# A spiking attention and a mixture of experts on one core: projections that begin with half of the tiles transposed, and a routing cut into parts

## The chip, the core and the metric

One core of one Trainium2 chip runs the whole program. The time is that of the device for one execution, in microseconds; where several runs are shown, their median counts. TensorE (PE in the profile) multiplies, VectorE (DVE), ScalarE (ACT) and GpSimd (POOL) do the elementwise work, and SyncE (SP) issues most of the transfers. Each engine goes through its own instructions in program order; semaphores tie the engines together.

## What is computed

The input is 2 x 2048 rows of 256 numbers. With `xn` the rows after a layer norm:

```python
x = L0_attn_query
xn = _layernorm(x, axis=-1)
x = x + _L0_attn_ref(xn, Wq, bq, ..., scale) + _L0_ffn_ref(xn, router_w, up_proj, down_proj)
```

The attention makes Q, K and V as spikes (1 where the layer norm of a projection is at least 1, else 0), weighs them by a Hamming distance and a bias by position, and makes spikes again after an output projection. The other branch routes each row to the 2 best of 8 experts by `xn @ router_w.T`, runs `silu(h[:256]) * h[256:]` and a down projection in each, and adds the two results, weighted.

## The kernel before

The 4096 rows are 32 tiles of 128 rows. The program goes through four stages.

**Prologue.** SP loads x in five chunks (`X_CHUNKS`: tiles 0-3, 4-7, 8-15, 16-23, 24-31). DVE takes means and variances of a chunk (`stats`), POOL the reciprocal deviation (`first_rstd`), DVE normalises the tiles in place (L807). PE transposes two tiles at a time (`turn_pair`, L1156) into one of four PSUM banks, ACT copies them out (`keep_xT`, L404). The router's logits are taken four tiles at a time, transposed (`logits`, L1168), copied (`keep_lgT`) and turned back (L1184). Beside this the four weight matrices `w_f` are prepared: POOL subtracts a base row (L646), ACT sums each half column block (`sum_weights`, L416), DVE subtracts the mean and multiplies by the sign of the gain (L828), and ACT and DVE split each number into an upper and a lower part (`w_h` L426, `w_l` L841), since every product is made of three matmuls (`three`, L1136 to L1138). The order is fixed: all 32 tiles are normalised, then the weights are signed, then the projections start.

**Projections.** Step t of 32 projects tile t to q, k and v: 3 groups of 6 matmuls (`project`). ACT takes the squares of each group (`squares`, L486) and, once for a pair of tiles, a square root (`deviations`, L492); DVE refines it (L988 to L994), makes six spikes (L1005) and splits the transposed tiles (`keep_xl`, L815; ACT's part is `keep_xh`). Four steps later PE turns tile t's q spikes (`turn_q`, L1202), ACT copies them (`keep_qT`, L478), and PE adds the product of k and v spikes to a bank (`sum_kv`, L1221). A PSUM bank holds two groups, and the pairs alternate between two sets of three banks.

Expert weights come in 24 pieces of 256 KB (`load_piece`, `ew_f`, two buffers); ACT writes a piece's upper part (L449), then POOL (the first 8, L643) or DVE (the others, L982) the lower part, which frees the buffer for the load after next.

**The routing** is DVE work ahead of the first pair's spikes: the best and second best expert (`pick` twice, L864 to L882), PE's counts and ranks by two matmuls, running counts and places (L887 to L919), then the gates (`set_gates`, L924 to L930) after the first pair. With places and gates set, POOL sends every tile's rows to two slots each in HBM: `scatter`, 64 indirect transfers (L683), each tile's pair waiting for the projections of three tiles on (`LEAD`). The rest of POOL's program stands behind them.

**Attention** runs over 16 blocks a of two tiles: PE sums near and far blocks, turns the spikes, and projects them; POOL takes a reciprocal deviation for each block (`out_rstd`, L703, and L687 for seven small scatters of padding between); DVE makes the output spikes (`spike_out`) and adds x (`add_x`). SP loads x again (`xo`, four slots, L354), loads the last ten pieces, and stores each block (`store_block`, L348); a slot is loaded again when its store has landed.

**Experts.** 71 tiles of 128 slots are loaded, projected up and down and added to the output by indirect transfers (L736).

The line that gates the scatters, and the loop behind it:

```python
            for t in range(NT):
                pool.wait_ge(s["proj_done"], G3 * min(t + LEAD, NT - 2))
                scatter(t)
            ...
            for a in range(NB):
                out_rstd(a)
```

## Time and profile before

| | us |
|---|---|
| median of 3 runs | 422.99 (421.54 to 424.07) |
| the profiled execution | 421.92 |
| its span | 420.1 |
| PE busy | 367.0 (87%) |
| DVE busy | 270.8 (64%) |
| POOL busy | 233.4 (56%) |
| ACT busy | 225.8 (54%) |

The profiled execution took 1.8 us more than its span and 1.07 us less than the median of the runs. Spans are counted from the first instruction; the busy times are sums over an engine's instructions and say nothing of what waits for what. For that the trace of each engine is read in order of time, with the start of each instruction in its first column.

### The profile page before, as it was taken

What the parts mean: (1) busy time and instruction counts of PE and PEld (TensorE: products, weight loads), DVE (VectorE), ACT (ScalarE), POOL (GpSimd) and SP (SyncE); (2) the same over time, 40 slices, a digit from 0 to 9 for tenths busy, and PEclk for the clock granted to TensorE, in tenths of its full rate; (3) what the DMA queues carried; (4) which work ended last, traced back from release to release, by engine and by line L of the source; (5) the groups of instructions that cost most, each with busy time, mean ns of one, the idle gap of its engine ahead of it and who ended that gap; (6) DMA issues with size and microseconds to landing.
All of it is one profiled execution on the core that took longest, in us unless ns stands there. A gap on an engine that the chain in (4) does not pass through costs nothing.

```text
span 420.1 us, 9186 instructions
## 1 busy us (share of the span) xinstructions
PE 367.0 (87%) x2429; PEld 297.0 (71%) x2430; DVE 270.8 (64%) x897; ACT 225.8 (54%) x716; POOL 233.4 (56%) x207
## 2 busy tenths in 40 slices
PE   5198876999999989998979999999999999999980
PEld 1033676888888847665767888888888788888860
DVE  4699799987777646757775555555555555555540
ACT  1456774777777645534454555555555555555540
POOL 4547424777777753542335755464755555555652
PEclk9689978999999999998999999999999999999995
DMA  7943012244626323557455757565666656565643
GB/s 258 322 153 75 26 50 65 102 154 128 206 103 217 113 90 114 190 189 219 133 162 171 114 97 110 91 103 99 101 101 101 99 90 97 96 100 94 104 52 37
DMA packets 43460, 51.72 MB, mean 123 GB/s; under 512 B 6342, under 2 KB 37064, under 8 KB 43432
## 3 DMA queue, kind: packets, MB, share of 16 engines
q0 software_dynamic: 13952, 19.30, 26.2%
q1 hardware_dynamic: 27488, 30.21, 24.1%
q10 hardware_dynamic: 1992, 1.89, 1.4%
q8 instruction: 12, 0.20, 0.2%
q14 instruction: 16, 0.13, 0.1%
HBM read 27.89 MB, written 23.48 MB: 122 GB/s over the span
## 4 chain that ended last, share of the span: by engine, by line
PE 51%; DVE 19%; DMA 14%; ACT 6%; issue 5%; SPq 1%; POOLq 0%; DVEq 0%; POOL 0%; ACTq 0%
PE bank L1136 14%; PE bank L1138 13%; PE bank L1137 13%; DMA out<-xo 7%; DMA xn<-x 3%; PE bank L1278 3%; DVE qk_spk L1005 3%; PE bank L1260 3%; DVE xn L807 2%; DMA ew_f<-experts 2%; ACT junk L486 2%; DVE xst L785 2%; PE bank L1312 2%; DMA ex<-slot_x 2%; DVE exT_l L974 2%
## 5 line engine op out<-in xcount | busy, mean ns | idle before, releaser
L736 POOL DMA_INDIRECT out<-ey,dest x71 | 110.0, 1549 | 78.9 <-DMA out<-ey,dest 24.4
L1036 DVE TENSOR_TENSOR hid<-gact,bank 128x256 f32<-128x256 f32 x71 | 29.9, 421 | 76.7 <-ACT gact L531 76.7
L683 POOL DMA_INDIRECT slot_x<-xn,pos x64 | 62.8, 982 | 25.7 <-issue 19.3
L1136 PE MATMUL bank<-ew,exT_h 128*128 x142 | 62.1, 437 | 6.4 <-DVE exT_l L974 6.2
L1136 PE MATMUL bank<-w_h,xT_h 128*128 128x256 f32 x192 | 58.9, 307 | 0.3 <-DVE w_l L841 0.3
L531 ACT ACTIVATE gact<-bank 128x256 f32<-128x256 f32 x71 | 27.3, 384 | 57.2 <-PE bank L1138 57.2
L1137 PE MATMUL bank<-w_l,xT_h 128*128 128x256 f32 x192 | 56.3, 293 | 0.0
L1138 PE MATMUL bank<-w_h,xT_l 128*128 128x256 f32 x192 | 56.1, 292 | 0.0
L1138 PE MATMUL bank<-ew,exT_l 128*128 x142 | 55.9, 394 | 0.0
L1137 PE MATMUL bank<-ew,exT_h 128*128 x142 | 55.8, 393 | 0.0
L486 ACT ACTIVATE junk<-bank 128x256 bf16<-128x256 f32 x96 | 35.9, 380 | 27.7 <-PE bank L1138 27.4
L1136 PE MATMUL bank<-ew,hidT_h 128*128 x142 | 46.0, 324 | 2.1 <-DVE hidT_l L1040 2.0
L541 ACT ACTIVATE hidT_h<-bank 128x256 fp32r<-128x256 f32 x71 | 27.2, 384 | 34.6 <-PE bank L1278 34.5
L1138 PE MATMUL bank<-ew,hidT_l 128*128 x142 | 40.3, 284 | 0.0
L1137 PE MATMUL bank<-ew,hidT_h 128*128 x142 | 40.2, 283 | 0.0
L1136 PEld LDWEIGHTS bank<-w_h,xT_h 128*128 128x128 f32 x192 | 38.7, 202 | 0.6 <-issue 0.4
L703 POOL TENSOR_TENSOR rstd<-veps,neg_half 128x2 f32<-128x2 f32 x16 | 17.0, 1061 | 39.6 <-DVE veps L1073 39.6
L1137 PEld LDWEIGHTS bank<-w_l,xT_h 128*128 128x128 f32 x192 | 38.8, 202 | 0.0
L1138 PEld LDWEIGHTS bank<-w_h,xT_l 128*128 128x128 f32 x192 | 38.8, 202 | 0.0
L1136 PEld LDWEIGHTS bank<-ew,exT_h 128*128 128x128 f32 x142 | 26.7, 188 | 13.7 <-issue 10.6
L547 ACT ACTIVATE ey<-bank,gate 128x256 f32<-128x256 f32 x71 | 33.2, 468 | 2.6 <-PE bank L1138 1.5
L1040 DVE TENSOR_TENSOR hidT_l<-bank,hidT_h 128x256 fp32r<-128x256 f32 x71 | 30.1, 424 | 6.6 <-ACT hidT_h L541 2.9
(203 smaller groups left out, 893.3 us busy)
## 6 DMA issues: line engine op xcount, KB each, us to landing
ex<-slot_x SPq DMA_DIRECT2D x71, 130.0 KB, 2.6
ew_f<-experts SPq DMA_DIRECT2D x24, 256.0 KB, 3.2
xo<-x SPq DMA_DIRECT2D x16, 256.0 KB, 3.0
out<-xo SPq DMA_DIRECT2D x16, 256.0 KB, 3.5
xn<-x SPq DMA_DIRECT2D x6, 512.0 KB, 12.6
out<-ey,dest POOLq DMA_INDIRECT x71, 3.9
xn<-x SPq DMA_DIRECT2D x4, 256.0 KB, 3.8
w_f<-w_all ACTq DMA_DIRECT2D x1, 1024.0 KB, 8.1
```

Of the source, the lines that this page charges most:

```text
L486: nc.scalar.activation(junk[:, i % JUNK, :], proj_ps[r][i], ACT.Square, accum_out=ssq[:, r, i:i + 1]).then_inc(s["ssq_done"], 1)
L531: nc.scalar.activation(gact[:, m % 2, :], h_ps[m % 2][:, 0:F], ACT.Silu).then_inc(s["gact_done"], 1)
L541: nc.scalar.activation(flat2(hidT_h[:, m % 2, :, :]), hT_ps[m % 2], ACT.Copy).then_inc(s["hidh_set"], 1)
L547: nc.scalar.activation(ey[:, m % 4, :], y_ps[m % 2], ACT.Copy, scale=gate[:, m % 4:m % 4 + 1]).then_inc(s["ey_done"], 1)
L683: pool.indirect_dma_start(slot_x, bass.IndirectOffsetOnAxis(ap=pos[:, k, t:t + 1], axis=0), xn[:, t, :], None).then_inc(s[done], 16)
L703: g.tensor_tensor(rstd[:, a % 2, 0:B], veps[:, a % 2, 0:B], neg_half[:, 0:B], ALU.pow).then_inc(s["w_rstd"], 1)
L736: pool.indirect_dma_start(out, bass.IndirectOffsetOnAxis(ap=dest[:, j:j + 1], axis=0), ey[:, j % 4, :], None, compute_op=ALU.add).then_inc ...
L1036: v.tensor_tensor(hid[:, m % 2, :], gact[:, m % 2, :], h_ps[m % 2][:, F:2 * F], ALU.mult).then_inc(s["hid_done"], 1)
L1040: v.tensor_tensor(flat2(hidT_l[:, m % 2, :, :]), hT_ps[m % 2], flat2(hidT_h[:, m % 2, :, :]).bitcast(F32), ALU.subtract).then_inc(s["hidl_ ...
L1136: mm(dst, a_h, b_h, start=first, stop=False)
L1137: mm(dst, a_h, b_l, start=False, stop=False)
L1138: return mm(dst, a_l, b_h, start=False, stop=last)
```

## The change

The prologue now turns 16 tiles only (`AHEAD = 8` pairs); pairs 8 to 15 are transposed and routed inside steps 1 to 4 of the projections, two pairs a step, all through one bank (6). DVE signs the weights in two halves between the chunks' statistics and subtracts the base itself; the signs are spread by one DVE instruction (128x1024) and two matmuls rather than a transfer. The normalisation of tiles 12-15, 20-23 and 28-31 goes to POOL, that of tiles 24-27 to ACT. The logits are taken for one tile at a time, with the transposed tile as the stationary side, straight into bank 7. The routing is cut into seven parts: with `PICKED = 2`, `pick_first` stands behind pair 2's spikes on DVE, `pick_second` behind pair 3's, `counts` behind pair 4's, `places` and `set_gates` behind pair 5's, the rest behind pairs 6 and 7. Bank 7 is used for the routing until then, so the key sums begin at step 15 with the first 12 tiles in two steps. The scatters have no wait of their own any more. DVE's refinement of the square root has three instructions in place of four. The pieces come in another order (`ORDER`, `PIECES_AT`).

```diff
-LGT_PIECE, BIAS_PIECE, RT_PIECE, XT_PIECE = 9, 13, 15, 17
+ROUTING_PIECES, BIAS_PIECE, RT_PIECE, XT_PIECE = range(9, 13), 13, 15, 17
+ORDER = [*range(POOL_PIECES), 8, 14, 16, 17, 18, 19, 9, 10, 11, 12, 13, 15, 20, 21, 22, 23]
...
-LEAD = 3
...
+PIECES_AT = {0: 0, 2: 1, 4: 2, 5: 3, 6: 4, 7: 5, 8: 6, 9: 7, 12: 8, 14: 9, 16: 10, 18: 11, 20: 12, 22: 13}
+LATE = [t for t, m in PIECES_AT.items() if m >= POOL_PIECES]
+ATTENTION_PIECES = {k: len(PIECES_AT) + k for k in range(PIECES - len(PIECES_AT))}
 FIRST_ROWS = 9
+AHEAD = 8
+PICKED = 2
+TURNS_FROM = 1
+OPENED = 15
+EARLY_K = 12
+POOL_NORM = [t for t in range(X_CHUNKS[2][0], NT) if t % 8 >= 4]
+ACT_NORM = [t for t in range(X_CHUNKS[4][0], NT) if t % 8 < 4]
...
+        x_ps = [banks[i % 4 if i < AHEAD else 6] for i in range(NT // 2)]
+        sgn_ps = [part(4 + g // 2, g % 2) for g in range(G4)]
+        lg_ps = banks[7][:, 0:NT * E]
...
+            for i in range(4):
+                keep_xT(i)
+            for i in range(KC * G4):
+                sum_weights(i)
+            act.wait_ge(s["bias_in"], 32)
+            sum_biases()
             halve_weights(1)
-            keep_lgT(NT // RG - 1)
+            keep_xT(4)
+            keep_xT(5)
+            halve_weights(0)
+            keep_xT(6)
+            keep_xT(7)
+            keep_xh(0)
+            keep_xh(1)
+            halve_out_weights()
+            halve_biases()
 
...
+                if 0 <= t - TURNS_FROM < 4:
+                    keep_xT(AHEAD + 2 * (t - TURNS_FROM))
+                    keep_xT(AHEAD + 2 * (t - TURNS_FROM) + 1)
...
+                if t in PIECES_AT:
+                    piece_upper(PIECES_AT[t])
                 if not even:
                     act.wait_ge(s["proj_done"], G3 * t + 3)
                     squares(t, 4)
-                    if t == 1:
+                    deviations(t)
...
+                if t == 1:
+                    normalise()
...
+            def normalise(c):
+                for t in [t for t in POOL_NORM if X_CHUNKS[c][0] <= t < X_CHUNKS[c][1]]:
+                    g.tensor_scalar(xn[:, t, 0:D], xn[:, t, 0:D], xmean[:, t:t + 1], xrstd[:, t:t + 1],
+                                    ALU.subtract, ALU.mult).then_inc(s["xn_pool"], 1)
...
+            set_ones(0)
+            set_ones(1)
+            for c in range(2, len(X_CHUNKS)):
                 first_rstd(c)
-            piece_lower(0, 0)
-            first_rstd(len(X_CHUNKS) - 1)
-            for n in range(1, POOL_PIECES):
-                if n < 4:
-                    set_ones(n - 1)
-                if n == 4:
-                    for group in range(3, NT // RG):
-                        set_ones(group)
-                    pool.wait_ge(s["w_halved"], 2 * KC)
-                    g.tensor_tensor(wo_l[:, :, :], w_f[:, :, G3 * D:], wo_h[:, :, :].bitcast(F32), ALU.subtract).then_inc(s["wo_parted"], 1)
-                piece_lower(n, n)
+                pool.wait_ge(s["xrstd_done"], c + 1)
+                if c == len(X_CHUNKS) - 1:
+                    offsets(c)
+                normalise(c)
+                if c == 3:
+                    set_ones(2)
+                    set_ones(3)
+            pool.wait_ge(s["wo_halved"], KC)
+            g.tensor_tensor(wo_l[:, :, :], w_f[:, :, G3 * D:], wo_h[:, :, :].bitcast(F32), ALU.subtract).then_inc(s["wo_parted"], 1)
+            piece_lower(0)
+            for group in range(4, NT // RG):
+                set_ones(group)
+            for m in range(1, POOL_PIECES):
+                piece_lower(m)
...
             for t in range(NT):
-                pool.wait_ge(s["proj_done"], G3 * min(t + LEAD, NT - 2))
                 scatter(t)
...
+            stats(0)
+            stats(1)
+            normalise(0)
+            normalise(1)
+            dve.wait_ge(s["w_in"], 16)
+            dve.wait_ge(s["base_in"], 16)
+            subtract_base(1)
+            dve.wait_ge(s["row0_gone"], 1)
+            subtract_base(0)
+            stats(2)
+            sign_weights(1)
+            normalise(2)
+            stats(3)
+            sign_weights(0)
...
+            for i, c in enumerate((1, 0)):
+                dve.wait_ge(s["w_halved"], i + 1)
+                v.tensor_tensor(w_l[:, c, :], w_f[:, c, 0:G3 * D], w_h[:, c, :].bitcast(F32), ALU.subtract).then_inc(s["w_parted"], 1)
...
+            normalise(3)
+            stats(4)
+            normalise(4)
+            keep_xl(2)
+            keep_xl(3)
...
+                for at, part_of_routing in enumerate((pick_first, pick_second, counts, places, set_gates, rest_of_routing, landings)):
+                    if pair == PICKED + at - (at >= 4):
+                        part_of_routing()
...
+                turned = AHEAD + 2 * (t - TURNS_FROM)
+                turning = TURNS_FROM <= t < TURNS_FROM + 4
+                if turning:
+                    turn_pair(turned)
+                    logits(turned - 1)
                 for i in range(t % 2 * G3, (t % 2 + 1) * G3):
+                    if turning and i % G3 == G3 - 1:
+                        turn_pair(turned + 1)
+                        logits(turned)
...
+                if t == TURNS_FROM + 4:
+                    logits(NT // 2 - 1)
+                for at in range(t - 3) if t == TURNS_FROM + 4 else range(t - 4, t - 3) if t > TURNS_FROM + 4 else ():
+                    turn_q(at, at)
...
+                if t == 2 * PICKED + 6:
+                    counts()
+                if t == 2 * PICKED + 8:
                     ranks()
-                if m == 4:
+                if t == OPENED:
                     open_kv()
-                if not early(t, 4):
-                    sum_kv(t - 4, m - 4)
+                first = (t - OPENED) * EARLY_K // 2 if t < OPENED + 2 else t - 4
+                for at in range(first, min(first + EARLY_K // 2, t - 3) if t == OPENED else t - 3) if t >= OPENED else ():
+                    sum_kv(at, at)
```

What stands where, word for word in program order, at three places. First DVE behind the spikes of a pair (`qk_spk`, `qT`, `v_spk` in L1005, now L1056, are the spikes; `xT_l` is `keep_xl`; `first`, `second`, `work`, `best` are the picks; `cnt` and `run_c` the counts, `slot_of` and `pos` the places). Before, the whole routing up to the places stands ahead of the first pair:

```order
L882 TENSOR_TENSOR gwork<-best 128x32
L815 TENSOR_TENSOR xT_l<-xT,xT_h 128x256 [waits xh_set]
L887 COPY cnt<-bank 128x256 [waits ranked]
...
L919 CAST pos<-pos_f 128x64 [waits dve_order]
L988 TENSOR_SCALAR veps<-ssq 128x6 [waits ssq_done,wo_parted,w_parted]
L990 RECIPROCAL inv_std<-std 128x6 [waits std_done]
...
L1005 SCALAR_TENSOR_TENSOR qk_spk<-thr_r,std,bank 128x256 x2
L924 TENSOR_SCALAR gwork<-gwork 128x32 [waits gate_exp,bias_set]
```

Now, behind the spikes of pair 5:

```order
L1056 SCALAR_TENSOR_TENSOR qk_spk<-thr_r,std,bank 128x256 [waits q_turned]
L1056 SCALAR_TENSOR_TENSOR qT<-thr_r,std,bank 128x256
L961 TENSOR_TENSOR slot_of<-bank,run_c 128x256 [waits dve_order,ranked]
...
L969 CAST pos<-pos_f 128x64 [waits dve_order]
L974 TENSOR_SCALAR gwork<-gwork 128x32 [waits gate_exp]
...
L980 TENSOR_TENSOR xn<-gwork,xn 128x32 [waits dve_order]
L1033 TENSOR_TENSOR ew<-ew_f,ew 128x512 [waits piece_h]
```

The places (`pos`) and gates moved from the first pair to the sixth.

Second, POOL ahead of and behind the 64 scatters. Before:

```order
L676 TENSOR_TENSOR wo_l<-w_f,wo_h 128x512 [waits w_halved]
L643 TENSOR_TENSOR ew<-ew_f,ew 128x512 [waits piece_h] x4
L683 DMA slot_x<-xn,pos 9088x260 [waits proj_done,gates_set,placed]
L683 DMA slot_x<-xn,pos 9088x260
L683 DMA slot_x<-xn,pos 9088x260 [waits proj_done]
```

Now:

```order
L691 TENSOR_TENSOR wo_l<-w_f,wo_h 128x512 [waits wo_halved]
L665 TENSOR_TENSOR ew<-ew_f,ew 128x512 [waits piece_h]
L672 MEMSET xT 1x4x128 [waits logits_done] x3
L672 MEMSET xT_v 1x2x128 [waits logits_done]
L672 MEMSET xT_q 1x2x128
L665 TENSOR_TENSOR ew<-ew_f,ew 128x512 [waits piece_h] x7
L702 DMA slot_x<-xn,pos 9088x260 [waits gates_set,placed]
L702 DMA slot_x<-xn,pos 9088x260 x63
L721 TENSOR_TENSOR rstd<-veps,neg_half 128x2 [waits w_var,pads_marked,pads_placed]
```

Four more memsets that wait for logits now stand between the first and the second piece, and the scatters wait only once.

Third, PE in step 1, between the groups of a tile (`id_f,xn` is a transposition, `w_rt,xT` the logits):

```order
L1188 MATMUL bank<-w_h,xT_l 128x256
L1220 MATMUL bank<-id_f,xn 128x128 [waits xn_done,xT_ready]
L1220 MATMUL bank<-id_f,xn 128x128
L1220 MATMUL bank<-id_f,xn 128x128 [waits xn_done]
L1220 MATMUL bank<-id_f,xn 128x128
L1228 MATMUL bank<-w_rt,xT 128x8 [waits xT_ready]
L1228 MATMUL bank<-w_rt,xT 128x8 x3
L1186 MATMUL bank<-w_h,xT_h 128x256
```

The second pair of each of these steps waits for ACT's copy of the first (`xT_ready`), which ACT does behind the squares of the group before it.

## Rows read from the trace of the kernel before

**Rows 1.** PE, first group of projection matmuls by line: min/median/max ns, first and last start.

```profile
L1136 PE MATMUL bank<-w_h,xT_h x192: 278/283/579, 50.0 to 147.2; 128*128 128x256 f32 x192
```

**Rows 2.** POOL's scatters: busy and idle by group; idle by cause; first scatter; first out_rstd.

```profile
L683 POOL DMA_INDIRECT slot_x<-xn,pos x64 | 62.8, 982 | 25.7 <-issue 19.3
...
  issue: 19.3, 47
...
71.46 1.09 POOL L683 DMA_INDIRECT slot_x<-xn,pos  x1 [5.24 <-issue]
...
162.37 0.73 POOL L703 TENSOR_TENSOR rstd<-veps,neg_half 128x2 f32<-128x2 f32 x1 [7.59 <-DVE veps L1073]
```

**Rows 3.** SP in the attention, timeline: first store of a block; last load of xo.

```profile
166.23 0.39 SPq L348 DMA_DIRECT2D out<-xo  x1
...
216.90 0.37 SPq L354 DMA_DIRECT2D xo<-x  x1
```

**Rows 4.** DVE in the prologue, timeline (start us, us).

```profile
16.66 2.71 DVE L785 BATCH_NORM_STATS2 xst<-xn 128x6 f32<-128x256 f32 x8 [3.72 <-DMA xn<-x]
...
20.42 1.38 DVE L807 TENSOR_SCALAR xn<-xn,xmean,xrstd 128x256 f32<-128x256 f32 x4
...
42.08 3.26 DVE L828 SCALAR_TENSOR_TENSOR w_f<-w_f,w_mean,sgn_r 128x256 f32<-128x256 f32 x8
...
48.76 0.96 DVE L841 TENSOR_TENSOR w_l<-w_f,w_h 128x768 fp32r<-128x768 f32 x1 [0.56 <-ACT wo_h L427]
```

**Rows 5.** PE, timeline: transpositions of four tiles; logits of four tiles.

```profile
39.21 1.09 PE L1156 MATMUL bank<-id_f,xn 128*128 128x128 f32 x8
40.23 1.88 PE L1168 MATMUL bank<-xT,w_rt 128*8 128x512 f32 x4
```

**Rows 6.** PE in a window of two us: busy (count), granted clock, DMA share, GB/s.

```profile
52.00:54.00 2.00, 2.00 (x12) 0.50 0.00 0
```

**Rows 7.** Steady steps: PE's turns of q; ACT's squares and its copy; two xT copies.

```profile
100.78 0.27 PE L1202 MATMUL bank<-id_b,qk_spk 128*128 128x128 bf16 x2 [0.51 <-DVE qk_spk L1005]
...
103.21 0.27 PE L1202 MATMUL bank<-id_b,qk_spk 128*128 128x128 bf16 x2
...
99.52 0.38 ACT L486 ACTIVATE junk<-bank 128x256 bf16<-128x256 f32 x1 [0.31 <-PE bank L1138]
...
100.25 0.38 ACT L478 ACTIVATE qT<-bank 128x256 bf16<-128x256 bf16 x1
...
26.72 1.25 ACT L404 ACTIVATE xT<-bank 128x512 f32<-128x512 f32 x2 [0.45 <-PE bank L1156]
```

**Rows 8.** Pieces: their load (KB, us to landing); POOL's lower parts, timeline.

```profile
ew_f<-experts SPq DMA_DIRECT2D x24, 256.0 KB, 3.2
...
53.66 2.52 POOL L643 TENSOR_TENSOR ew<-ew_f,ew 128x512 fp32r<-128x512 f32 x2 [2.80 <-ACT ew L449]
```

**Rows 9.** DVE, timeline: a later pair without routing, its first and last group.

```profile
88.51 0.17 DVE L988 TENSOR_SCALAR veps<-ssq 128x6 f32<-128x6 f32 x1
...
91.45 0.87 DVE L1005 SCALAR_TENSOR_TENSOR qk_spk<-thr_r,std,bank 128x256 bf16<-128x256 f32 x2
```

**Rows 10.** DVE, timeline: the routing's parts, by their first and last instructions.

```profile
51.48 0.42 DVE L864 TENSOR_REDUCE best<-bank 128x32 f32<-128x256 f32 x1
...
58.31 0.42 DVE L815 TENSOR_TENSOR xT_l<-xT,xT_h 128x256 fp32r<-128x256 f32 x1
59.06 0.42 DVE L887 COPY cnt<-bank 128x256 f32<-128x256 f32 x1 [0.33 <-PE bank L1194]
...
64.63 0.38 DVE L919 CAST pos<-pos_f 128x64 int32<-128x64 f32 x1
...
70.34 0.22 DVE L930 TENSOR_TENSOR xn<-gwork,xn 128x32 f32<-128x32 f32 x1
```

**Rows 11.** ACT, timeline: the table load ahead of a square root, and the root.

```profile
58.67 1.28 ACT L492 ACT_TABLE_LOAD   x1
59.97 0.30 ACT L492 ACTIVATE std<-ssq,eps_c 128x6 f32<-128x6 f32 x1
```

More of the change, by code:

```diff
@@ L1146, in _, with wait_normal @@
             pe.wait_ge(s["ident_in"], 16)
+            pe.wait_ge(s["ones_set"], 1)
+            pe.wait_ge(s["sgn_put"], 1)
+            signs = sgn_w[:, :, :].rearrange("p a j -> p (a j)")
+            for h in range(2):
+                last = mm(banks[4 + h][:, :], ones_b[:, :], signs[:, h * G4 * D // 2:(h + 1) * G4 * D // 2], start=True, stop=True)
+            last.then_inc(s["sgn_set"], 1)
+            def wait_normal(t):
+                for who, done in ((POOL_NORM, "xn_pool"), (ACT_NORM, "xn_act")):
+                    if t in who:
+                        pe.wait_ge(s[done], who.index(t) + 1)
+                        return
+                pe.wait_ge(s["xn_done"], t + 1 - sum(n < t for n in POOL_NORM + ACT_NORM))
             def turn_pair(i):
-                if i >= 4:
+                if i > AHEAD:
+                    pe.wait_ge(s["xT_ready"], i)
+                elif 4 <= i < AHEAD:
                     pe.wait_ge(s["xT_ready"], i - 3)
@@ L1187, in ranks @@
-            def ranks():
-                pe.wait_ge(s["const_in"], 32)
-                pe.wait_ge(s["ones_set"], 1)
-                pe.wait_ge(s["chosen_set"], 1)
-                picks = chosen[:, :, :].rearrange("p t e -> p (t e)")
-                mm(rank_ps[:, 0:NT * E], before_s[:, :], picks, start=True, stop=True)
-                mm(rank_ps[:, NT * E:], ones_b[:, :], picks, start=True, stop=True).then_inc(s["ranked"], 1)
+            for i in range(4):
+                turn_pair(i)
+                if i >= 1:
+                    logits(i - 1)
@@ new lines, in _, with counts @@
+            logits(3)
+            for i in range(4, AHEAD):
+                turn_pair(i)
+                if i >= 5:
+                    logits(i - 1)
+            def counts():
+                pe.wait_ge(s["const_in"], 32)
+                pe.wait_ge(s["chosen_set"], 1)
+                mm(lg_ps, ones_b[:, :], chosen[:, :, :].rearrange("p t e -> p (t e)"), start=True, stop=True).then_inc(s["counted"], 1)
+            def ranks():
+                pe.wait_ge(s["counts_kept"], 1)
+                mm(lg_ps, before_s[:, :], chosen[:, :, :].rearrange("p t e -> p (t e)"), start=True, stop=True).then_inc(s["ranked"], 1)
```

363 lines of the change are left out of this document (162 added, 201 removed).

## The prediction

> **What bounds the kernel now.** I read the chain of waits first: it goes through DVE's prologue, then through PE and DVE in the projections, then through SP's stores in the attention, then through PE in the experts. Next I read each engine in order of time around the three seams between stages. The first projection starts at 50.0 us and the last group at 147.2 [rows 1]. Whatever happens before is prologue, and this change is about the prologue. But the row that decides is POOL's. Its 64 scatters start at 71.5. Their busy time is 62.8 and the idle time before them 25.7, of which 5.24 stands ahead of the first: 62.8 + 25.7 - 5.24 = 83.3 us from the first start to the last end, 154.8 [rows 2]. POOL's next work is the first `out_rstd` of the attention at 162.37, 7.6 us later, and DVE releases it, not POOL. So the scatters have 7.6 us to spare, no more. From there SP carries the end: the first block is stored at 166.23, and each of the following blocks waits until a slot's store has landed, until the last load of x at 216.90 [rows 3]. The experts stand behind that and nothing in them changes. So the time moves by as much as `out_rstd` of block 0 moves: it needs both the end of the projections (147.2 + 15.2 = 162.4) and the end of the scatters.
>
> **The start of the projections.** Before, statistics of chunk 2 start at 16.66, when its x has landed, and take until 20.42: 3.76 us for 8 tiles; four normalisations take 1.38 [rows 4]. DVE now has the spread of the signs, eight normalisations and two subtractions ahead of these statistics. By hand the spread costs 1.2 us (an estimate, from 0.96 for 768 columns [rows 4] to 1024) and each subtraction about that 0.96; with POOL's memset between them it all fits before 17.4. Then, in DVE's order: statistics 3.8, signs of one half 1.9 (8 took 3.26 [rows 4], and two small steps), normalisation of four tiles 1.4, statistics 3.8, signs 1.9, bias 0.6, two lower parts 1.9, one `keep_xl` 0.4. 17.4 + 15.7 = **33.1** for the first projection, 16.9 us earlier than 50.0. ACT's sums and copies and PE's 16 transpositions lie beside this. POOL normalises four tiles in between: no row shows that instruction; half of a 128x512 lower part is 0.63, twice of it 2.5 [rows 8], and even at 2.5 each the four end at 33, just in time.
>
> **Steps 0 to 5.** A step is 18 matmuls, a turn of q and two key sums: 103.21 - 100.78 = 2.43 us [rows 7], thus some 0.12 for a matmul, 0.72 for a group, 2.16 for a tile. Early in the projections of before, the granted clock was 0.50, 1.2 in place of 2.4 GHz, with 12 matmuls started in 2 us [rows 6]; step 0 now starts behind some idle microseconds of PE, and I take that level for most of it. Tile 0 then takes 3.5. In steps 1 to 4 PE adds two pairs of transpositions at 0.55 (8 in 1.09) and two logits. These are a new form: four matmuls of 8 columns against a 128x128 tile. From below they cost nothing beyond loads like the transpositions', 0.5; from above four of the old form, 1.88 [rows 5]; I take 0.5, since the load is the same and the moving side is small. More costly is the wait in the middle. The second pair goes into the same bank as the first, so it waits for ACT: end of a group 0.3, two squares 0.73 (99.52 to 100.25), one copy 0.6 (two in 1.25) [rows 7], with two hand-overs 1.8. An odd step has one group before that, an even one two: 0.55 + 0.5 + 0.72 + 1.8 + 0.55 + 0.5 + 0.72 = 5.3 and 6.1. Four steps: 22.8. Step 5 opens with one logits and two turns of q, the second behind ACT's copy of the first: 3.5. So tile 5 is done at 33.1 + 3.5 + 22.8 + 3.5 = 62.9, and a further 0.8 for ACT's own four normalisations. Its root is set 1.4 later, at 65.1.
>
> One more thing is queued. SP's load of piece 3 waits for POOL's lower part of piece 1, which now stands behind memsets that wait for the last logits, in step 5 (about 60.5). Memset, lower part 1.3, load 3.2, upper part 0.6 [rows 8]: ACT gets to the end of that piece at about 66.5, and two squares and the root of pair 2 stand behind it on ACT, 1.0: **67.5** in place of 65.1.
>
> **From there to the gates.** DVE now has more than PE. A pair without routing costs it 3.7 us (88.51 to 92.3 less the instruction dropped [rows 9]). Pairs 2 to 5: 14.8. The two picks cost 6.8 (51.48 to 58.31), counts and places 5.6 (59.06 to 65.0, less the `keep_xl` inside), the gates 1.0, ended by 70.34 before [rows 10]. Together 28.2, so the gates are set at 67.5 + 28.2 = **95.7**. PE's 2.43 a tile would take 20 us for the eight tiles, so PE waits for DVE there. In the kernel before the same point was 71.5 [rows 2]: the projections start 17 us earlier, the scatters 24 us later.
>
> **The scatters** no longer wait for projections. 17 of 64 did; their idle time was 25.7 - 19.3 = 6.4, of which 5.1 is the gap of 0.3 that all others have too (19.3 for 47, 5.24 of it the first [rows 2]). So 83.3 - 1.3 = 82.0 us at least. 95.7 + 82.0 = 177.7, against 162.4: **15.3 later**. The projections end earlier than before, near 144 (tile 13 at 91, 18 more at 2.8 as from 50.0 to 147.2 minus the slow start, 3 for the key sums moved), which would have let block 0 go at 159, but it now waits 18 us for POOL.
>
> **After the wait** the block's other work is ready, which saves 0.9 between `out_rstd` and its store (3.9 before, 162.37 to 166.23). PE is held at block 2's output projection and may come back at half clock [rows 6] for some us, which costs about 1 on block 2's store. DVE's chain for the root has still three instructions behind ACT's root; one is dropped that was done in ACT's shadow: nothing. SP's chain behind the first store is bound by stores that land, and is the same. Sum: 421.9 + 15.3 - 0.9 + 1 = 437.3 for an execution like the profiled one, which lies 1.07 under the median of the runs. I say **437**.
>
> **A rule weighed.** ACT's exponential for the gates now stands between the roots of pairs 4 and 5, so a table is loaded for it and one for the next root. The row shows 1.28 for a load and the root begins at 59.97, right behind its end at 59.95 [rows 11]. The root of pair 5 then comes just as DVE gets to it, and the sum is as above. The Trainium skill, "ScalarE: Activation LUTs", section "What ACT_TABLE_LOAD costs", gives 1283 ns for the load and about 1380 ns of drain besides. By that rule the root would come 1.4 later and the gates about 1 us later, and the time with them; the trace disagrees on the drain.
>
> **Rivals.**
> 1. *Faster: POOL issues quicker than it did.* If the gap between scatters goes with the waits, each takes its 0.98 and 64 take 63. Then they end at 159, the end of the projections decides, and the time is 422 - 3 = 419. It decides from a pace under 1.03 us each, (162.4 - 95.7) / 64. Against it: 47 scatters that waited for nothing had the gap [rows 2]. A faster routing alone gives little: even at PE's pace throughout (tile 5 at 56, eight tiles in 20, root and routing 5) the gates come at 81, with no gain at all. Chance 0.13, for both together.
> 2. *No change.* The gates come at 79 to 82: steps 1 to 4 without the wait for ACT (-7), the piece in time (-2.4), the picks at less (-1), and DVE's routing in gaps of its own. Too many at once: 0.07. The time would be 421 to 425.
> 3. *Much slower.* The half clock comes back after each of the waits of 1 to 2 us in steps 1 to 13, since PE is idle a quarter of that time. With tiles at 3.8 in place of 2.16 for half of ten tiles, the gates are 8 later: 445. Against it: steps with a gap of 0.51 ran at full speed, 2.43 [rows 7]; what wider gaps do, no row here shows. Chance 0.15.
> 4. *The forecast*, POOL's scatters as the bound with gates from 88 to 101: 0.65, 429 to 443.
>
> **Numbers.** The difference that a measurement can tell from none is 0.5%, 2.1 us. Faster by more: rival 1, 0.13. Within: 0.07. Slower: 0.80. The range must leave out no more than 2 in 10: it starts at 426, above rivals 1 and 2, which hold 0.2, and goes to 446, through rival 3.
>
> **What would show it.** First projection near 33; steps 1 to 4 near 5.3 and 6.1 with PE waiting on ACT's xT; scatters from 95 to 177 with no waits; the first reciprocal of the attention right behind the last scatter, PE idle some 15 us before; SP's chain from first store to last load still about 51. If POOL idles before its first `out_rstd`, or the first scatter is before 82, the forecast is wrong.

## The result, and the profile after

The changed kernel takes **445.95 us** (median of 4 runs, 444.31 to 449.89); the kernel before, beside it, 423.38. The ratio is 1.055, 95% interval 1.047 to 1.063. (Ratios here are those on record, taken over the executions of the faster of two states and not from the medians, so they can differ from the medians' quotient by up to 0.004.) The direction was forecast, the size was not: 437.0 was said, with a range to 446.0. The time just fills it, and the ratio applied to the 422.99 from which the forecast started gives 446.4, just above it. In a second comparison it took 445.79 against 422.67, ratio 1.052 (1.046 to 1.058). The profiled execution has a span of 443.1 us (444.92 with what lies around it).

The page's busy shares and granted clock, in 40 slices of 11.1 us:

```profile
PE   6878779688799983199797999999999999999971
POOL 3289615206777777746234565556565555555652
PEclk9557998999999999589999999999999999999995
```

In slices 16 and 17 (from 166 us) PE sinks to 3 and 1 while POOL goes on at 7: PE has finished the projections and waits. The groups of POOL's scatters and of PE's projections (times: min/median/max ns, first and last start us):

```profile
L702 POOL DMA_INDIRECT slot_x<-xn,pos x64 | 63.7, 995 | 37.9 <-issue 19.2
...
L702 POOL DMA_INDIRECT slot_x<-xn,pos x64: 956/960/1470, 101.4 to 183.3; - x64
...
L1186 PE MATMUL bank<-w_h,xT_h x192: 278/283/561, 35.7 to 150.4; 128*128 128x256 f32 x192
```

Against [rows 2] the scatters start at 101.4 in place of 71.5, and the last starts at 183.3, 29.5 us later than before (153.8); against [rows 1] the projections start 14.3 earlier and end 3.2 later. So more than the whole head start is gone by their end. The chain that ended last, at the seam (start us, us):

```profile
183.31 0.96 POOL slot_x L702
184.29 0.74 POOL rstd L721
185.03 0.19 issue
185.22 1.04 POOL slot_x L706
```

The first `out_rstd` (L721) stands at 184.29, right behind the last scatter and with no wait for DVE, whose `veps` for it was there at 167.3. Before, it stood at 162.37 behind 7.59 us of idle time. SP's loads and stores in the attention, first and last start:

```profile
L360 SPq DMA_DIRECT2D xo<-x x16: 367/368/442, 160.8 to 238.2; - x16
...
L354 SPq DMA_DIRECT2D out<-xo x16: 383/445/1218, 187.3 to 244.3; - x16
```

From first store to last load of x it is 50.9 us, as before (50.7 [rows 3]). ACT between the root of pair 0 and the routing (the roots are L504):

```profile
46.24 0.30 ACT L504 ACTIVATE std<-ssq,eps_c 128x6 f32<-128x6 f32 x1
...
58.96 0.30 ACT L504 ACTIVATE std<-ssq,eps_c 128x6 f32<-128x6 f32 x1
...
69.99 0.63 ACT L464 ACTIVATE ew<-ew_f 128x512 fp32r<-128x512 f32 x1 [1.36 <-DMA ew_f<-experts]
...
71.38 0.30 ACT L504 ACTIVATE std<-ssq,eps_c 128x6 f32<-128x6 f32 x1
...
91.81 1.28 ACT L504 ACT_TABLE_LOAD   x1
93.10 0.30 ACT L504 ACTIVATE std<-ssq,eps_c 128x6 f32<-128x6 f32 x1
```

and DVE's last steps to the gates:

```profile
99.31 0.19 DVE L969 CAST pos<-pos_f 128x64 int32<-128x64 f32 x1
...
100.26 0.22 DVE L980 TENSOR_TENSOR xn<-gwork,xn 128x32 f32<-128x32 f32 x1
```

The picked pair's root comes at 71.38 and the gates are set at 100.5. That is the forecast's chain, each link later than it was said.

### The profile page after: what moved, and what is told of

The parts are those of the page before. It is cut to its first block, busy times and chain, and to the rows that moved or that the text cites. A ratio compares the mean times of both kernels' runs of the same rounds, so it can differ in the third digit from the quotient of the medians.

```text
span 443.1 us, 9273 instructions
## 1 busy us (share of the span) xinstructions
PE 373.7 (84%) x2483; PEld 316.0 (71%) x2492; DVE 263.4 (59%) x870; ACT 223.6 (50%) x712; POOL 246.8 (56%) x218
## 4 chain that ended last, share of the span: by engine, by line
PE 46%; POOL 19%; issue 13%; DVE 10%; ACT 4%; DMA 4%; POOLq 0%; SPq 0%; ACTq 0%; DVEq 0%
POOL slot_x L702 14%; PE bank L1186 13%; PE bank L1188 11%; PE bank L1187 11%; PE bank L1228 3%; POOL rstd L721 3%; PE bank L1347 3%; PE bank L1329 3%; PE bank L1220 2%; DMA ex<-slot_x 2%; POOL slot_x L706 2%; DMA out<-xo 2%; DVE exT_l L1024 1%; ACT gact L543 1%; DVE xst L807 1%
## 5 line engine op out<-in xcount | busy, mean ns | idle before, releaser
L754 POOL DMA_INDIRECT out<-ey,dest x71 | 109.6, 1544 | 80.6 <-ACT ey L559 24.4
L702 POOL DMA_INDIRECT slot_x<-xn,pos x64 | 63.7, 995 | 37.9 <-issue 19.2
L1186 PE MATMUL bank<-ew,hidT_h 128*128 x142 | 46.2, 325 | 2.0 <-DVE hidT_l L1090 2.0
L721 POOL TENSOR_TENSOR rstd<-veps,neg_half 128x2 f32<-128x2 f32 x16 | 17.0, 1061 | 31.6 <-DVE veps L1123 31.6
```

Of the source, the lines that this page charges most:

```text
L702: pool.indirect_dma_start(slot_x, bass.IndirectOffsetOnAxis(ap=pos[:, k, t:t + 1], axis=0), xn[:, t, :], None).then_inc(s[done], 16)
L721: g.tensor_tensor(rstd[:, a % 2, 0:B], veps[:, a % 2, 0:B], neg_half[:, 0:B], ALU.pow).then_inc(s["w_rstd"], 1)
L754: pool.indirect_dma_start(out, bass.IndirectOffsetOnAxis(ap=dest[:, j:j + 1], axis=0), ey[:, j % 4, :], None, compute_op=ALU.add).then_inc ...
L1186: mm(dst, a_h, b_h, start=first, stop=False)
```

## The experiments

### Is the late end of the scatters the whole loss?

**g3_lead15** takes the kernel *before* and delays nothing but its scatters:

```
-LEAD = 3
+LEAD = 15
```

> The kernel before, with one number changed: scatters of tile t wait for projection step t + 15 instead of t + 3, so that POOL's last scatter ends where the changed kernel's does (184.3 instead of about 155). Nothing else of the change is in it. Forecast's theory (the late end of POOL's scatters is the whole loss): out_rstd(0) at 184 to 186, time 443 to 447, ratio 1.05 to 1.055, as the changed kernel. Rival (scatters late is only a part, the rest is lost in the changed kernel's waits and clock): 430 to 438.

Measured: 444.39 against 422.81, ratio 1.051 (1.049 to 1.053). The first `out_rstd` came at 186.1 and the last load of x at 238.6, where the changed kernel has 238.2. A kernel with none of the change's edits, only with POOL's scatters as late, is as slow. Not to the microsecond: its `out_rstd` stands 1.8 us behind the changed kernel's and its median 1.5 below, so some 3 of the changed kernel's 22.6 us come from elsewhere. The rest of what the other edits gain and lose lies beside POOL.

**f0_after** is the changed kernel again, beside the three that follow.

> The changed kernel, unchanged, beside the kernel before. In the first comparison the ratio was 1.055. In the batch before this one three variants of it stood at 1.11 to 1.13 of the kernel before on the same chip, with TensorE and ScalarE idle for tens of us while POOL issued its scatters, and the wait ending on nothing that the profile shows. Theory A (the variants' edits do it): this run shows 1.055 and no such idle time. Theory B (it is a state of the chip, and hits whatever kernel has projections still to fetch beside scatters): on a chip with it this run too stands at 1.10 to 1.13; on a chip without it, 1.055.

Measured: 445.79, ratio 1.052 (1.046 to 1.058). By itself that fits both theories. What speaks against A is that e1_between's and e4_lump's very edits, which stood at 1.115 and 1.129, stand at 1.054 and 1.035 in the same comparison as this run (f1_between and f2_lump). Its profile comes below.

### Taking POOL off the path, and starting it earlier

**f1_between** puts the last 7 tiles' scatters and the pads between the first blocks' `out_rstd`:

```
+BESIDE = 7
...
-            for t in range(NT):
+            for t in range(NT - BESIDE):
                 scatter(t)
...
                 out_rstd(a)
-                if a < PC:
-                    scatter_pad(a)
+                if a < BESIDE:
+                    scatter(NT - BESIDE + a)
+                elif a < BESIDE + 3:
+                    for c in range(PC * (a - BESIDE) // 3, PC * (a - BESIDE + 1) // 3):
+                        scatter_pad(c)
```

> The changed kernel with its last 7 scatters of tokens, and then the pad rows' scatters, put between out_rstd(0) to out_rstd(9) on POOL instead of before out_rstd(0). Theory forecast (POOL's scatters end last): without stalls out_rstd(0) goes from 184.3 to about 170, and the time falls by 13 to 17 us, to about 0.965 to 0.97 of the changed kernel. Rival (expert loop waits for the last pads, so that the scatters are the bound wherever they stand): no change within 3 us.

Measured: 445.24 against 422.67, ratio 1.054 (1.050 to 1.058): nothing gained, although the first `out_rstd` stood at 168.8, 15.5 us earlier. SP's waits from 150 to 262 us (total, times, longest) tell why:

```profile
SPq L361 <- DMA out<-xo: 35.1, 11, 5.1
...
SPq L369 <- DMA slot_x<-pad_row,pad_i: 12.6, 1, 12.6
```

In block 9 SP waits for *all* scatters and pads before it loads the first slots, and the later blocks' loads of x are queued behind that wait. It stood there 12.6 us, and each of the six blocks left took a store's landing. The rival had the result right, with this queue as its reason.

**g1_between5** moves 5 tiles in place of 7, and that wait (`FIRST_ROWS`) from block 9 to 11.

> The changed kernel with its last 5 tiles of scatters (10 of 64) and the pad rows' scatters put between out_rstd(0) and out_rstd(7), and SP's wait for all scatters moved from block 9 to block 11, since in the run before (7 tiles, wait at 9) SP stood 12.6 us at that wait and the rest of the blocks went at 3.6 us each behind it. Theory (POOL's scatters end last, and SP's wait took back the gain): out_rstd(0) at about 172 instead of 184.3, the last load of xo at 228 or 229 instead of 238.2, time 9 to 10 us below the changed kernel. Rival (all of POOL's work has to be done before the expert loop wherever it stands): within 3 us of it.

Measured: 436.59 against 422.81, ratio 1.033 (1.030 to 1.037), 9 us less. `out_rstd` of block 0 at 171.4, last load of x at 229.2: the theory's numbers. Two things changed at once against f1_between; that the moved wait is the one that counts is read from SP's waits, in which none for the pads is left.

**f2_lump** leaves the scatters alone and has the whole routing in one piece behind step 7:

```
-                    if pair == PICKED + at - (at >= 4):
+                    if pair == PICKED + max(0, at - 4):
...
-                if t == 2 * PICKED + 6:
+                if t == 2 * PICKED + 3:
                     counts()
-                if t == 2 * PICKED + 8:
                     ranks()
```

(on ACT, the exponential goes from `2 * PICKED + 5` to `+ 3`.)

> The changed kernel with the routing not in parts: three routing steps (counts and ranks too) stand right behind step 7 instead of spread to step 12. On the disturbed chip the first scatter came at 93.8 instead of 101.4. Theory (start of the scatters sets the end): 7 to 9 us less, 437 for 446, as all that stands behind POOL's chain moves with it. Rival (what the projections lose by the lump comes back at the end): less than 3 us.

Measured: 436.85 against 422.67, ratio 1.035 (1.031 to 1.038), 9 us less. First scatter 93.1 for 101.4, first `out_rstd` 174.9 for 184.3.

**f3_both** and **g2_both5** join the lump with f1_between's and g1_between5's edits; f3_both has POOL's memsets of g4_ones (below) besides.

> Lump and between together, and POOL's memsets for groups 4 on behind the lower pieces of the experts' weights instead of before them. Theory: POOL is off the chain; out_rstd(0) then follows the projections (end at 150 + 15, 166 to 168), and the time is 424 to 430, about the kernel before, not below it, since step 1 still begins 15 us early and loses it at waits. Rival (start stretch given back): 415 to 420.

> The same with the routing in one lump, which alone gave 9 us. Theory: both gains add, out_rstd(0) at 165 to 167 (projections' end 152 + 15 is then as late), time 421 to 428, level with the kernel before. Rival: the two share one gain, 434 to 437.

Measured: 446.56, ratio 1.057 (1.052 to 1.063), and 436.03, ratio 1.028 (1.025 to 1.030). g2_both5 came out as its rival said: the gains share one limit. f3_both hit neither span (424 to 430, 415 to 420): SP stood 12.7 us at the same wait for the pads as in f1_between. ACT's last root of the projections in the changed kernel, in the lump, and in g2_both5:

```profile
L504 ACT ACTIVATE std<-ssq,eps_c x16: 298/299/302, 46.2 to 151.8; 128x6 f32<-128x6 f32 x16
```

```profile
L504 ACT ACTIVATE std<-ssq,eps_c x16: 298/299/301, 46.3 to 159.2; 128x6 f32<-128x6 f32 x16
```

```profile
L505 ACT ACTIVATE std<-ssq,eps_c x16: 298/299/303, 46.7 to 162.1; 128x6 f32<-128x6 f32 x16
```

The lump starves PE for DVE's 14 us of routing and ends the projections 7 to 10 us later. Alone that costs nothing, since POOL ends at 174.9 anyway; with POOL taken off the path the projections decide, and `out_rstd` of block 0 is back at 175.9, behind 10.5 us in which POOL waits for DVE. (The profiled execution of g2_both5 took 439.56, 3.5 more than the median; PE's granted clock was 0.50 to 0.66 in it from 50 to 62 us.)

### The steps ahead of the gates

**g4_ones** moves POOL's memsets for the later logits behind its lower parts (behind all eight of them; what counts is that pieces 1 and 2 are among these).

> The changed kernel, with POOL's memsets of the ones of groups 4 on put behind the lower parts of pieces 1 and 2 instead of before them, so that piece 3 lands earlier: ACT waited 1.36 us for it at 69.99, in the middle of the steps before the root of pair 2. Theory (the forecast's step on piece 3): the root of pair 2 and all behind it 1.4 to 2 us earlier, time 1 to 2 us less, ratio 1.047 to 1.051. Rival (the pair's root hangs on TensorE's steps alone): no change within 1 us.

Measured: 444.07 against 422.81, ratio 1.051 (1.047 to 1.056): inside the theory's span and, with this interval, no less inside the rival's. The trace decides: ACT's wait for piece 3 is gone and the root of pair 2 stands at 70.64 for 71.38, of which 0.27 was there at pair 0; ACT waits 0.93 for PE in its place. The late piece was real and worth half a microsecond.

**h1_picked1** sets `PICKED = 1`.

> The changed kernel with PICKED = 1 instead of 2: the routing's parts each stand one pair of steps earlier. Forecast's step (gates = root of the picked pair + 28.2, and all behind follows): a pair is 6 us, first scatter at 95 to 96 instead of 101.4, time 5 to 6.5 us below the changed kernel (439 to 441). Rival (the routing waits then for something else, as logits of the last tiles or the router's copies): first scatter moves by less than 3 us, and so does the time.

Measured: 440.26 against 422.32, ratio 1.041 (1.038 to 1.044), 5 us less, as the theory says; but in the profiled execution, the longest of its five, the first scatter came at 100.8, as the rival says. PE's clock was at half there from 50 to 60 us, which it was not in the changed kernel's profile. The time is measured; the way to it is not shown by this trace. h4_best's, below, has the first scatter at 97.8, 3.6 earlier, part of which is g4_ones' edit: less than the 5 to 6 of the theory.

**h2_warm** keeps PE busy in the prologue with 16 matmuls that nobody reads.

> The changed kernel with 16 matmuls 128x512 in the transposing stretch whose result nobody reads, to keep TensorE busy while it waits (6 before the transposes of pair 4, 4 before those of pair 6, 6 before step 0). Theory (TensorE's half clock from 12 to 38 us makes the late start): the granted clock is 1.00 before 30 us and the first projection comes 2 to 3 us earlier, at 33, time 2 to 3 us less. Rival (DVE and POOL set the pace there; the matmuls add or hide): the first projection stays at 35.6 within 1 us, the time within 1.5.

Measured: 447.43, ratio 1.060 (1.057 to 1.062). PE ran at 0.91 to 0.94 from 26 to 34 us, where it had 0.50, and the first projection came at 36.8, not at 35.7. The theory's 33 did not come, but that does not clear PE's clock. The clock rose too late: DVE's wait of 1.3 us for `xrstd`, which hangs on PE's logits (the first point under Wrong, below), was over at 24.4 and is as long as before. And the last six of the added matmuls themselves stand in front of the first projection, at a clock of 0.50 again (34 to 38 us). L1301 is their line, of which the trace has five:

```profile
34.97 2.34 PE bank L1301 x5
```

What the half clock costs at the start is not settled by this run.

**h3_dvenorm** sets `POOL_NORM = []`, so that DVE does all of POOL's normalisations.

> The changed kernel with the normalisation of all tiles on DVE (and ScalarE as before), none on POOL; DVE gets 12 more operations of 0.34 us, POOL loses 12 of 1.2 to 1.9 us (and one of 3.9). Theory (POOL's normalisation is on the path of the start): first projection 2 us earlier, time 2 us less. Rival (DVE is as full as POOL there, and gets 4 us more): first projection as late or later, time the same or 1 to 2 us more.

Measured: 454.17, ratio 1.076 (1.073 to 1.079), 9 us more: further than the rival said. The start is only 1.9 later (37.6). The profile is that of the longest of the six executions (461.93), and what PE's clock did in it comes next. The five others have no trace; their mean granted clock was 0.905 to 0.921, the changed kernel's four had 0.918 to 0.930. Where the median's further 7 us came from is open.

**h4_best** joins `PICKED = 1`, the memsets behind the pieces, and g1_between5's order.

> PICKED = 1, the memsets of ones behind the pieces, and the last 5 tiles' scatters and the pads' between out_rstd(0) and out_rstd(7). Theory: out_rstd(0) comes from 171.4 to the end of the projections + 15, 166 to 167, time 428 to 432; still above the kernel before, since the projections end 3 us later than its own (150.3 for 147.2) and the last blocks' loads keep their pace. Rival: POOL's remaining work bounds it again, 434 to 437.

Measured: **430.43** against 422.32, ratio 1.018 (1.014 to 1.022), the best version of the changed kernel. First scatter 97.8. The first `out_rstd` still stands right behind a scatter:

```profile
166.68 0.17 DVE L1126 TENSOR_SCALAR veps<-ssq 128x2 f32<-128x2 f32 x1 [1.61 <-ACT junk L587]
...
166.74 0.96 POOL L702 DMA_INDIRECT slot_x<-xn,pos  x1 [0.30 <-issue]
...
167.71 0.76 POOL L721 TENSOR_TENSOR rstd<-veps,neg_half 128x2 f32<-128x2 f32 x1
```

DVE's `veps` was there at 166.9, so without the scatter it would have gone some 0.6 us earlier. Both limits have come together: 167.7 is 16 us behind the last group of the projections (151.8), and in the kernel before, 162.4 is 15 behind 147.2. The projections end 4.6 later than there, and the last load of x comes 5.6 later (222.5).

### A spell at half clock

f0_after's profiled execution, the longest of its four, is the same program as the changed kernel's, but its span was 453.3, not 443.1. Windows of 4 us (busy time and count of PE, PEld, DVE, ACT, POOL; granted clock), first of the 443.1 us execution, then of the 453.3 us one, then of h3_dvenorm:

```profile
46.00:50.00 4.00, 2.09 (x18) 1.89 (x17) 0.13 (x1) 3.97 (x13) 4.00 (x5) 1.00 0.00 0
50.00:54.00 4.00, 3.93 (x35) 3.93 (x36) 3.90 (x11) 1.44 (x4) 1.84 (x3) 1.00 0.22 70
...
66.00:70.00 4.00, 3.96 (x23) 3.90 (x23) 3.29 (x3) 1.84 (x8) 2.44 (x2) 0.57 0.34 79
70.00:74.00 4.00, 3.21 (x29) 3.04 (x27) 2.18 (x8) 3.78 (x14) 1.41 (x2) 1.00 0.33 110
```

```profile
46.00:50.00 4.00, 2.76 (x24) 2.55 (x22) 0.00 (x0) 3.93 (x13) 4.00 (x4) 1.00 0.00 0
50.00:54.00 4.00, 3.27 (x17) 3.27 (x18) 3.36 (x9) 2.10 (x6) 2.13 (x3) 0.65 0.19 70
54.00:58.00 4.00, 4.00 (x21) 4.00 (x20) 1.43 (x4) 0.00 (x0) 0.51 (x1) 0.50 0.00 0
...
82.00:86.00 4.00, 3.36 (x30) 3.19 (x29) 3.55 (x11) 2.96 (x12) 0.99 (x2) 1.00 0.24 70
```

```profile
46.00:50.00 4.00, 1.62 (x11) 1.42 (x11) 3.94 (x9) 3.00 (x10) 2.45 (x2) 0.65 0.13 16
50.00:54.00 4.00, 4.00 (x20) 4.00 (x20) 2.16 (x6) 0.41 (x1) 0.51 (x1) 0.50 0.14 49
...
78.00:82.00 4.00, 4.00 (x21) 3.80 (x20) 0.00 (x0) 0.00 (x0) 0.10 (x1) 0.50 0.00 0
```

In the second the clock fell to 1.2 GHz behind ACT's four normalisations (46 to 50 us, in which PE waits) and stayed there until 82. PE starts some 20 matmuls in 4 us there where it starts up to 35 at full clock, and DVE and ACT stand idle for lack of work. The roots of pairs 0, 1 and 2 come at 46.9, 64.7 and 82.0 for 46.2, 59.0 and 71.4, the first scatter at 112.6 for 101.4, and the span is 10.2 longer. So the difference arises in this stretch, beside the clock. These are two single executions: why the clock fell in one and not in the other is not shown. In h3_dvenorm's the clock fell in the same place and was back only behind 86 us: first scatter 118.5. The kernel before has such windows too [rows 6], but its scatters started at 71.5 with 7.6 us to spare at the end.

### Two comparisons in which engines stood idle

The first four runs (e1 to e4) and the last two (i1, i2) fell in conditions under which the kernel before itself took 452.2 and 448.4 us; their times aren't comparable with the others, and only their traces up to the scatters are used.

> Theory (POOL's 64 scatters stand ahead of the first out_rstd and set the end): with the last seven tiles' scatters put behind out_rstd of blocks 0 to 6, block 0 waits for the end of the projections only, 150.4 + 15.2 = 166 in place of 184.3; time 446 - 18 = 428, up to 431 if POOL is then busy in every block. Rival (the projections lose the time themselves, the scatters only end at about the same moment): block 0 goes at 183 as before and the time stays within 1 of 446. Nothing but POOL's order is changed.

> The kernel before, with each tile's scatters held until 16 tiles on are projected in place of 3. Theory: the first scatter moves from 71.5 to about 93, the last ends 82 later at 175 in place of 154.8, the 7.6 of slack are used up, and out_rstd of block 0 goes at 175 to 176; time 422 + 13 = 435. Rival (the end of the projections decides and scatters are hidden): 423, within 0.5%.

> The changed kernel, with ACT copying a step's first pair ahead of the squares instead of behind them, so that PE's second pair in steps 1 to 4 does not wait. Theory: each of the four steps is 1.5 to 1.8 shorter, the root of pair 2 is 5 to 6 earlier, and so are the gates, the scatters and the end: 440. Rival (DVE or the piece queue behind the last logits decides, not this wait): 445 to 446.

> The changed kernel, with picks, counts, places and gates in one piece behind pair 2's spikes. Theory: the 28 us from the root to the gates lose three pairs' own work (3 x 3.7), so the gates come at 90 in place of 100.5 and the time is 435 to 436, although PE starves once for some 9 us. Rival (the end of the projections decides): PE's long wait costs as much as the short ones or more, 446 to 449.

Measured: 505.08, 472.79, 505.95 and 510.58 against 452.24. e1 and e4 are f1 and f2 above; e2 is g3 with 16 for 15. A window of e3 in the midst of the scatters:

```profile
140.00:150.00 10.00, 0.00 (x0) 0.00 (x0) 0.00 (x0) 0.00 (x0) 7.56 (x9) 0.50 0.29 107
```

POOL scatters at its pace while PE, DVE and ACT have no instruction at all from 130 to 160 us, and PE is busy for 1.9 us in the 50 from 120 to 170. What PEld waits for in i1, from 95 to 240 us:

```profile
PEld bank L1258 <- issue: 72.1, 5, 51.6
```

The wait ends on nothing that the profile shows, and what it is, no run here shows. It does not come with the scatters alone: f0 to h4, whose programs have the same scatters (h1 to h4 ran on the very chip of e1 to e4), had none of it. None of the times expected for these runs, i1 and i2 among them, came, and they say nothing for or against the theories.

e3 and i1 test the wait in the middle of steps 1 to 4, by ACT's first copy of xT ahead of the squares; i1 has g4's memsets besides, and i2 has `PICKED = 1` and g1's order too.

```
+                if 0 <= t - TURNS_FROM < 4:
+                    keep_xT(AHEAD + 2 * (t - TURNS_FROM))
                 if even:
```

> The changed kernel with ACT's first copy of xT of steps 1 to 4 ahead of the squares instead of behind them, and POOL's memsets of ones behind the lower parts of pieces 1 and 2, so that piece 3 is no longer late. Theory (the wait in the middle is on the path, and piece 3 hid its gain in the earlier run): root of pair 2 at 68 to 70 instead of 71.4, first scatter 2 to 3.5 us earlier, time 2 to 3.5 less than the changed kernel (ratio 1.045 to 1.048). Rival (TensorE's clock and work set the steps): first scatter within 1 us of 101.4, ratio 1.050 to 1.055.

> The same with PICKED = 1 and the last 5 tiles' scatters and the pads' between out_rstd(0) and out_rstd(7): the combination that gave 430.4, plus ACT's copies first. Theory: out_rstd(0) bound by the projections' end + 15, so 1 to 3 us less than that, 427.5 to 429.5. Rival: no change, 430 to 431. Below the kernel before (422.5) it does not come in either.

Measured: 503.62 and 494.00 against 448.38. In e3 the root of pair 2 came at 71.07, behind a wait of 1.85 us for piece 3. In i1, without that wait, at 68.77 for 71.38, and the first scatter at 99.5 for 101.4. Between e3 and i1 the piece is worth 2.3 us at the root, where it was worth half a microsecond alone (g4_ones). What the wait in the middle costs is not separated: PE's granted clock was 0.64 and 0.50 (e3), 0.60 and 0.55 (i1) in the two windows from 50 to 58 us and 1.00 from 66 to 70, where the changed kernel's had 1.00 and then 0.57. The whole, 2.6 us at the root and 1.9 at the scatters, is a little less than the theory. What it brings in time, and whether i2 beats 430.4, stays open.

## Why the prediction was right and wrong

**Right**: the mechanism and its place. [Rows 2]'s 7.6 us to spare, the 64 scatters without waits, PE idle at the seam, `out_rstd` right behind the last scatter, SP's chain of 51 us; g3_lead15 shows it to be the loss, all but some 3 us. Rival 1's condition did not come: the gap of 0.3 stayed (19.2 for 63), at 1.27 each. The store of block 0 came 3.0 us behind its `out_rstd`, the 0.9 less that was said. The table load had no drain behind it (91.81 + 1.28, root at 93.10) and none ahead of it (ACT's instruction before ended at 91.79). There the trace again disagrees with the Trainium skill's "ScalarE: Activation LUTs", section "What ACT_TABLE_LOAD costs".

**Wrong**: the size. The first `out_rstd` moved by 21.9, not 15.3. The steps that failed are terms of the sum up to the first scatter, by the table:

| step | forecast | measured | miss, summed |
| --- | --- | --- | --- |
| first projection | 33.1 | 35.7 | 2.6 |
| root of pair 2 | 67.5 | 71.4 | 3.9 |
| gates set | 95.7 | 100.5 | 4.8 |
| first scatter | 95.7 | 101.4 | 5.7 |
| end of the last scatter | 177.7 | 184.3 | 6.6 |

1. *The start of the projections*, 2.6 of 6.6, the largest. The forecast added up DVE's work, gave its hand-overs no time, and said that ACT's and PE's work "lie beside this". They don't. DVE's waits until then are:

```profile
DVE xn L829 <- POOL xrstd L650: 1.3, 1, 1.3
DVE w_f L833 <- POOL w_r L678: 0.8, 1, 0.8
DVE w_mean L837 <- ACT junk L426: 0.6, 1, 0.6
```

   The 0.8 lies ahead of the statistics of chunk 2, which start at 17.59 for 17.4: 0.2 of it counts. Behind them DVE's work took the 15.7 that were said, and the waits 0.6 and 1.3. A last 0.5 is PE's: DVE's first `xT_l` was ready at about 35.2, and PE was at its last logits until 35.7. The chain in order of time:

```profile
19.80 3.23 PE bank L1228 x16
...
23.07 0.51 POOL xT L672
23.59 1.61 POOL xrstd L650
...
25.23 1.61 DVE xn L829 x4
...
33.42 0.49 ACT xT L410
...
33.96 1.88 PE bank L1228 x8
```

   So the wait of 1.3 is one of order: POOL's memset of ones (L672) stands ahead of `xrstd` and waits for PE's logits, while DVE's variances for `xrstd` were there at 21.4. PE's granted clock was 0.50 from 14 to 38 us, and the logits of a pair took 1.7 there, 0.8 at 1.00 (39.88 to 40.69). Both waits on PE thus hang on its clock, by this trace; no run tests it, since h2_warm raised the clock too late, and none moves this memset. POOL's normalisations are not the cause: the four that were bounded at 2.5 us each took 1.2 each and ended at 30.3, and h3_dvenorm starts later without them.
2. *Steps 0 to 5*, 1.3. PE at the starts of step 1, of its logits and first group, of step 5, of its first group, and of step 6:

```profile
39.44 0.60 PE L1220 MATMUL bank<-id_f,xn 128*128 128x128 f32 x4
39.88 0.96 PE L1228 MATMUL bank<-w_rt,xT 128*128 128x8 f32 x8
40.69 0.36 PE L1186 MATMUL bank<-w_h,xT_h 128*128 128x256 f32 x1
...
64.39 0.96 PE L1228 MATMUL bank<-w_rt,xT_q 128*128 128x8 f32 x8
...
66.12 0.37 PE L1186 MATMUL bank<-w_h,xT_h 128*128 128x256 f32 x1
...
69.84 0.30 PE L1258 MATMUL bank<-id_b,qk_spk 128*128 128x128 bf16 x2
```

   Steps 1 to 4 took 25.0 for 22.8 + 0.8, step 5 took 5.5 for 3.5, step 0 a further 0.3. The logits of a pair were put at 0.5 and took 0.8, and step 5's 18 matmuls took 3.7 at clock 0.57, for 2.16. Against that the late piece was put at 2.4 and cost almost nothing: the root came 1.5 behind the end of tile 5, where the forecast had 1.4 without the piece, and taking the piece away gave half a microsecond (g4_ones). So 3.6 too little and 2.3 too much cancel in part, which is luck.
3. *Root to gates*, 29.1 for 28.2: DVE waited 1.2 for the root behind the second table load, which the sum had "just as DVE gets to it".
4. *The hand-over to POOL*, 0.9, between the gates at 100.5 and the first scatter at 101.4, was left out altogether, though the kernel before shows the same 0.9 (70.34 + 0.22 [rows 10], first scatter 71.46 [rows 2]); the scatters took 82.9 for 82.0.
5. *The end of the projections* was said to come near 144 and came at 150.4. That does not set the time here, since POOL's end is later, but it does bound what h4_best can gain.

Behind the seam 1.0 more was lost than said (profiled execution 444.92; 437.3 + 6.6 = 443.9): block 2's store cost its 1.0 and more (1.6), the later blocks won most of that back, and behind the last load of x it took 204.9 us to the end for 203.2 before, in a stage in which nothing was to change; why is not shown. The median lies 1.0 above the profiled execution; the forecast had named the same 1.07 of the kernel before and not added it. Together that is the 9 (6.6 + 1.0 + 1.0, and 0.3 by rounding down).

Rival 3, the half clock behind waits, had 0.15 and 445. It was a wrong picture as a rival: it does not replace the forecast, it comes on top of it. In the profiled execution it took parts (0.57 from 66 to 70 us, 0.61 from 86 to 90); the longest execution of the second comparison, with a spell of 30 us at half clock, was 10 us longer. The range, closed at 446 by counting it as the farthest case rather than adding it to the forecast's own 443, was too narrow upwards.

## What to carry to other kernels

An engine with a long list of indivisible work (64 scatters at 1.27 us) has a latest start; a change that starts another stage 14 us earlier but moves this start by 30 is paid in full once the slack of 7.6 is used up. Read that slack first, from the idle time ahead of the next work on the same engine. Before work is moved behind such a wait, look at the in-order queues behind it: 15 us gained at POOL vanished at one wait in SP's queue; with the wait moved as well (and 5 tiles in place of 7) 9 of 13 came through. When work is added up for one engine, look also at what stands ahead of each hand-over in the other engines' order: a memset that waits for PE held up a reciprocal that did not need it, and with it DVE. And two edits that each give 9 us need not give 18: look at what ends second.

## What the runs showed of the hardware

- In one execution TensorE was busy for 2.9 to 4.0 of each 4 us from 54 to 82 us and its granted clock stayed at 0.50 (1.2 GHz). In another of the same program it was 1.00 there but for 66 to 70 us (0.57); that one was 10 us shorter.
- Ahead of the fall PE was busy for 2.76 of 4 us at 1.00, and the next window had 0.65; in the other execution it was busy for 2.09 of the same 4 us, and the clock stayed at 1.00. These rows give no rule for it.
- POOL's normalisation of a 128x256 tile took 1.2 us where DVE takes 0.40 in the same kernel: eleven of twelve, with DVE busy beside them or not. One took 3.9, beside DVE's lower parts of the weights; why is not shown.
- A scatter by POOL took 0.96 us at the median (1.47 at most) with a gap of 0.30 behind it, in all 63 gaps of the changed kernel, and POOL kept that pace in the stretch of e3 in which the other engines stood.
- A table load on ACT took 1.28 us, with no idle time ahead of it or behind it that the trace shows (91.79, 91.81, 93.10).
- PE, DVE and ACT stood without work for 30 us and more beside indirect DMAs in two of six comparisons, and in those the variants of the changed kernel stood at 1.10 to 1.13 of the kernel before, where the same or like edits stood at 1.02 to 1.05 elsewhere.
